# Layer 1's way in by token halves, idle products on TensorE, and two scan pairs of WKV 1 at another place

## The reference

```python
ek = exp(min(k, 30)); ekv = ek * v          # k = v = fside, the same for all layers
a = a * decay + ekv_t; b = b * decay + ek_t # scan over tokens, forward and in reverse
num = nf + nb - ekv + euk * vf              # euk = exp(min(u + k, 30))
den = df + db - ek + euk
out = sigmoid(r) * (num / max(den, 1e-8)) * (0.8 + 0.2 * tf)   # r = x
```

## Time and profile before

| | us |
|---|---|
| median of 3 runs (519.27 to 520.88) | 520.41 |
| profiled execution | 519.72 |
| its span, first to last instruction | 517.8 |
| PE busy | 437.8 (85%) |
| DVE busy | 377.9 (73%) |
| ACT busy | 195.2 (38%) |
| POOL busy | 108.0 (21%) |
| mean granted PE clock | 0.924 of 2.4 GHz |

### The profile page before, as it was taken

The page is one execution under the profiler, slowest core; times in us unless marked ns, Lnnn a source line. Parts: engine busy times, 40 slices in busy tenths (PEclk is TensorE's granted clock), DMA queues, the critical chain, the costliest instruction groups (busy, mean ns, idle before and its releaser), DMA issues.

```text
span 517.8 us, 5641 instructions
## 1 busy us (share of the span) xinstructions
PE 437.8 (85%) x2006; PEld 269.3 (52%) x2006; DVE 377.9 (73%) x663; ACT 195.2 (38%) x339; POOL 108.0 (21%) x65
## 2 busy tenths in 40 slices
PE   0796789987670899999999999999999999987572
PEld 0342444776470377899998997534434434322120
DVE  4999888797899798768666686375566773347975
ACT  4450155652221486321544824250010030146481
POOL 0000000000000297322000000047466654350000
PEclk9998788998965599999999999899999999999695
DMA  7910000710192127744754239020000000000001
GB/s 294 416 48 1 1 0 0 288 69 1 43 327 76 44 53 234 236 130 162 203 184 160 85 128 332 6 84 0 0 0 1 1 0 0 0 0 1 1 26 55
DMA packets 12093, 47.76 MB, mean 92 GB/s; under 512 B 2866, under 2 KB 5147, under 8 KB 9763
## 3 DMA queue, kind: packets, MB, share of 16 engines
q1 hardware_dynamic: 10914, 43.48, 24.0%
q0 software_dynamic: 1152, 3.93, 3.1%
HBM read 45.04 MB, written 2.37 MB: 92 GB/s over the span
## 4 chain that ended last, share of the span: by engine, by line
PE 69%; DVE 22%; issue 3%; ACT 3%; DMA 3%; SPq 0%; DVEq 0%
PE bank L1417 9%; PE bank L1391 8%; PE bank L1506 7%; PE bank L1515 7%; PE bank L1426 5%; PE bank L1543 3%; PE bank L1546 3%; PE bank L1279 3%; DMA const<-in_const 3%; PE bank L1321 2%; PE bank L1340 1%; PE bank L1311 1%; PE bank L1482 1%; DVE arena L903 1%; PE bank L1383 1%
## 5 line engine op out<-in xcount | busy, mean ns | idle before, releaser
L568 ACT ACTIVATE early<-bank 128x512 f32<-128x512 f32 (+1 forms) x24 | 14.3, 596 | 98.5 <-PE bank L1515 90.4
L1133 DVE TENSOR_TENSOR early<-early,bank 128x512 f32<-128x512 f32 (+1 forms) x24 | 16.4, 684 | 48.0 <-ACT early L568 47.6
L1391 PE MATMUL bank<-onehot,rows 128*128 128x512 f32 x192 | 51.4, 406 | 0.0
L341 POOL DMA_INDIRECT arena<-token_rows,arena x24 | 35.6, 1484 | 70.4 <-DVE arena L921 36.9
L1417 PEld LDWEIGHTS bank<-arena 128*96 128x96 f32 x512 | 44.2, 165 | 4.0 <-issue 3.9
L1506 PE MATMUL bank<-cT,arena 128*128 128x512 f32 (+1 forms) x96 | 46.2, 606 | 0.0
L1515 PE MATMUL bank<-arena 128*128 128x512 f32 (+1 forms) x96 | 45.8, 596 | 0.1
L1417 PE MATMUL bank<-arena 128*96 128x48 f32 x512 | 44.8, 248 | 0.3 <-issue 0.3
L1391 PEld LDWEIGHTS bank<-onehot,rows 128*128 128x128 f32 x192 | 33.9, 189 | 6.1 <-DVE onehot L952 0.3
L354 POOL TENSOR_TENSOR early<-early,arena 128x512 f32<-128x512 f32 (+1 forms) x12 | 28.0, 2333 | 41.8 <-DVE early L1133 41.8
L352 POOL TENSOR_TENSOR early<-early,arena 128x512 f32<-128x512 f32 (+1 forms) x12 | 15.1, 1262 | 103.0 <-DMA arena<-pair_weights 98.1
(11 more groups left out here) (315 smaller groups left out, 869.2 us busy)
## 6 DMA issues: line engine op xcount, KB each, us to landing
arena<-in_w_gate SPq DMA_DIRECT2D x8, 768.0 KB, 4.8
arena<-in_w_up SPq DMA_DIRECT2D x8, 768.0 KB, 7.8
arena<-in_w_down SPq DMA_DIRECT2D x8, 768.0 KB, 9.5
const<-in_const SPq DMA_DIRECT2D x1, 2122.5 KB, 13.1
arena<-in_wq SPq DMA_DIRECT2D x1, 2048.0 KB
arena<-in_wo SPq DMA_DIRECT2D x1, 2048.0 KB, 9.3
kT<-in_kT SPq DMA_DIRECT2D x2, 512.0 KB, 5.3
xT<-in_xT SPq DMA_DIRECT2D x1, 1024.0 KB, 8.5
```

What stands on the lines that cost most here:

```text
L341: g.indirect_dma_start(xg[:, t % XRING, :], None, scratch[:, :], bass.IndirectOffsetOnAxis(ap=toki[:, t:t + 1].bitcast(U32), axis=0)).then ...
L1391: return mm(bank[2 * ct + ch][:], rows1[:, i % RRING, part, ct * P:(ct + 1) * P], onehot1[:, t, ch * CHUNK:(ch + 1) * CHUNK], start=False, ...
```

## The change

- `scalar`: `gate(l)` becomes `gate0()` (as before) and `gate1()`, which makes four sigmoids of 512 columns, token half by token half, each as soon as its addition is done.
- `vector`: `cond(1)` (two products of 1024 columns behind the four additions) becomes four `cond1(i)` of 512 columns; the first stands behind the third addition, the others behind the fourth. The additions go by token halves. `ratio_ready` is waited for ahead of them.
- `tensor`: the scatter goes by token halves; two idle products of 512 columns into bank 5 follow it. The logits wait for `c_ready` 2 for tokens 0 to 511 and 4 for the rest, instead of for all at once; the wait for `x1_ready` stands behind the logits.
- `tensor`: three idle products into bank 6 behind the QKV bias products; the definition of `idle` moves to the block's head.
- `vector`: `num_scans(1, 0, 0)` and `(1, 0, 1)` move from in front of the selected rows' copy to behind `den(1, 1)`.
- `vector`: the residual `x1` is added straight from bank 4, and the copy `ao` is made behind its sum of squares.
- Layer 2's waits on `sig_ready` and `c_ready` count two more.

```diff
--- before.py
+++ after.py
@@ -395,13 +395,17 @@
-            def gate(l):
+            def gate0():
+                act.wait_ge(S("x_in"), 16)
                 for ct in range(CT):
-                    if l == 0:
-                        act.wait_ge(S("x_in"), 16)
-                    else:
-                        act.wait_ge(S(f"x{l}_ready"), 2 * ct + 2)
                     s.activation(cT[:, ct, :], xT[:, ct, :], ACT.Sigmoid).then_inc(S("sig_ready"), 1)
...
+            def gate1():
+                for i in range(4):
+                    ch, ct = divmod(i, 2)
+                    cc = slice(ch * CHUNK, (ch + 1) * CHUNK)
+                    act.wait_ge(S("x1_ready"), i + 1)
+                    s.activation(cT[:, ct, cc], xT[:, ct, cc], ACT.Sigmoid).then_inc(S("sig_ready"), 1)
@@ -424,7 +428,7 @@
             euk(0)
-            gate(0)
+            gate0()
             for j in range(4):
@@ -474,7 +478,7 @@
-            gate(1)
+            gate1()
             act.wait_ge(S("logit1_done"), 1)
@@ -667,11 +671,11 @@
-            def cond(l):
-                dve.wait_ge(S("ratio_ready"), l)
-                for ct in range(CT):
-                    dve.wait_ge(S("sig_ready"), 2 * l + ct + 1)
-                    v.tensor_tensor(cT[:, ct, :], cT[:, ct, :], ratio[l % 2][:, ct, :], ALU.mult).then_inc(S("c_ready"), 1)
+            def cond1(i):
+                ch, ct = divmod(i, 2)
+                cc = slice(ch * CHUNK, (ch + 1) * CHUNK)
+                dve.wait_ge(S("sig_ready"), CT + i + 1)
+                v.tensor_tensor(cT[:, ct, cc], cT[:, ct, cc], ratio[1][:, ct, cc], ALU.mult).then_inc(S("c_ready"), 1)
@@ -744,8 +748,6 @@
             den_sum(1, 1)
-            num_scans(1, 0, 0)
-            num_scans(1, 0, 1)
@@ -771,6 +773,8 @@
             den(1, 1)
+            num_scans(1, 0, 0)
+            num_scans(1, 0, 1)
             cosb = cs[:, 0:64].unsqueeze(1).to_broadcast([P, 8, 64])
@@ -817,9 +821,9 @@
             dve.wait_ge(S("wo_done"), 1)
-            step(v.tensor_copy(ao, bank[4][:, 0:C]))
-            step(v.tensor_tensor(x1, xs, ao, ALU.add))
+            step(v.tensor_tensor(x1, xs, bank[4][:, 0:C], ALU.add))
             sumsq(x1, 6)
+            v.tensor_copy(ao, bank[4][:, 0:C])
             dve.wait_ge(S("rms0"), 2)
@@ -843,13 +847,17 @@
+            dve.wait_ge(S("ratio_ready"), 1)
             for i in range(4):
-                ct, ch = divmod(i, 2)
+                ch, ct = divmod(i, 2)
                 dve.wait_ge(S("scatter0_done"), i + 1)
                 xx = xT[:, ct, ch * CHUNK:(ch + 1) * CHUNK]
-                v.tensor_tensor(xx, xx, bank[i][:], ALU.add).then_inc(S("x1_ready"), 1)
...
-            cond(1)
+                v.tensor_tensor(xx, xx, bank[2 * ct + ch][:], ALU.add).then_inc(S("x1_ready"), 1)
+                if i == 2:
+                    cond1(0)
+            cond1(1)
+            cond1(2)
+            cond1(3)
             last_tokens(wD)
@@ -1045,7 +1053,7 @@
                     cc = slice(ch * CHUNK, (ch + 1) * CHUNK)
-                    dve.wait_ge(S("sig_ready"), 2 * CT + 2 * ct + ch + 1)
+                    dve.wait_ge(S("sig_ready"), 3 * CT + 2 * ct + ch + 1)
                     v.tensor_tensor(cT[:, ct, cc], cT[:, ct, cc], ratio[0][:, ct, cc], ALU.mult).then_inc(S("c_ready"), 1)
@@ -1199,6 +1207,11 @@
+            def idle(bk, n):
...
+                for _ in range(n):
+                    mm(bank[bk][:], ident, iota[:, 0:CHUNK], start=True, stop=True)
...
             def tokens_to_rows(banks, layer):
@@ -1243,6 +1256,7 @@
                 qkv_bias(j)
+            idle(6, 3)
             pe.wait_ge(S("rank_ready"), 1)
@@ -1327,19 +1341,20 @@
             pe.wait_ge(S("dl_ready"), 1)
-            for ct in range(CT):
-                for ch in range(NCH):
+            for ch in range(NCH):
+                for ct in range(CT):
                     mm(bank[2 * ct + ch][:], dl[:, ct * P:(ct + 1) * P], onehot[:, ch * CHUNK:(ch + 1) * CHUNK],
...
-            pe.wait_ge(S("c_ready"), 2)
-            pe.wait_ge(S("x1_ready"), 4)
+            idle(5, 2)
             pe.wait_ge(S("small1_in"), 80)
             for i in range(NT):
+                pe.wait_ge(S("c_ready"), i // 4 * 2 + 2)
                 for ct in range(CT):
...
             last.then_inc(S("logit1_done"), 1)
+            pe.wait_ge(S("x1_ready"), 4)
             tokens_to_rows([0, 1, 2, 3], 1)
@@ -1435,11 +1450,6 @@
                 last.then_inc(S("outtr_done"), 1)
...
-            def idle(bk, n):
...
-                for _ in range(n):
-                    mm(bank[bk][:], ident, iota[:, 0:CHUNK], start=True, stop=True)
@@ -1582,11 +1592,11 @@
             pe.wait_ge(S("w2a_in"), 112)
-            pe.wait_ge(S("c_ready"), 3)
+            pe.wait_ge(S("c_ready"), 5)
             z2(0, 0)
...
             for half in range(2):
-                pe.wait_ge(S("c_ready"), 5 + half)
+                pe.wait_ge(S("c_ready"), 7 + half)
                 logits2(half)
```

## The result

| | before | changed |
|---|---|---|
| median | 519.99 us (4 runs, 519.27 to 520.88) | 530.63 us (4 runs: 523.58, 530.35, 530.92, 532.79) |
| profiled execution, its span | 519.72, 517.8 | 530.92, 528.6 |
| mean granted clock | 0.924 | 0.906 |
| PE busy | 437.8 (85%) | 449.2 (85%) |

The ratio is 1.0162 [1.0117, 1.0207]; forecast were 516.3 us and a range of 514.2 to 518.9. Ratios leave out runs over 1.5% above a kernel's fastest as disturbed; here that upper level is itself what the change brings, so I also give medians over all runs, and how many lie at 526 us or above.

A forecast was written before the change was run, and what follows sets the result against it. It took PE (69%) and DVE (22%) alternating up to 183 us, then nearly all PE, as the bound. 3.2 + 0.3 + 0.87 - 0.3 = 4.1 us off 519.72 gave 515.6, median 516.3; range 514.2 to 518.9.

The forecast's parts named there:

- what is won earlier moves that part as a block: From 183 us on, nearly all PE and unedited: time won earlier shifts this whole part with it.
- PE early wins nothing there and PE late costs: At 183 us, gather and shared products' end coincide: earlier PE gains nothing, each us of later clock rise costs 0.5.
- Bounds 0 and 3.6: Loss if the clock rises later under the last eight shared passes at 183 us: 0 to 3.6 us, taken as 0.3.
- rival (c): Early idle products late and QKV at 1.2 GHz beyond 5.6 us: slower, 522.2 us at 10 us; chance 0.06.
- The early idle products: In PE's hole before the rank product: clock holds, one-hots start 0.2 us earlier, row selection 0.8 us shorter.
- the bound named beside it: Early idle products at 1.2 GHz: they take 5.1 us, end at 60.9, and everything on DVE is 2.8 later.
- Rival (b): Early idle products don't hold the clock: 520.0 us at worst, 518 with most at 2.4 GHz; chance 0.17.
- The scans: Two WKV 1 scan pairs moved: with the early idle products 3.2 us gained up to attention, between 2.2 and 4.2.
- The residual: Layer 0, add reads the bank, its 0.42 us copy moves behind: gain 0.3 us, between 0 and 0.42.
- The way in: Scatter to layer 1's routing: logits 3.5 us instead of 6.99, stage gains 0.87 us, bounds 0.5 and 0.9.
- The pieces: Layer 1 gating on DVE: two 512-column pieces cost what one of 1024 did, against the skill's some 0.3 us more.

The follow-up runs named there:

- c2: Changed kernel plus twelve idle products: seven before the routing weights' wait, three at the expert loop's entry, one in each of the first two groups; median 524.40 us.
- i1: e2_no_early plus twelve idle products: seven before the routing weights' wait, three at the expert loop's entry, one in each of the first two groups; median 519.92 us.
- s1_scans: Kernel before, with only the two scan pairs moved and the residual read from the bank; median 517.22 us, ratio 0.9947.
- s3_early: Kernel before, with only the three idle products behind the bias products added; median 534.19 us.
- e2_no_early: Changed kernel without the three idle products ahead of the rank product; median 527.93 us.
- t1_wait1: e2_no_early with the routing's first addition done twice, 0.75 us more; median 517.37 us, ratio 0.9939.

## Why the prediction was wrong, point by point

- **The step that failed:** "what is won earlier moves that part as a block", said of all that comes behind 183 us, and with it "At 183 the first gather and PE's shared products arrive together …, so PE early wins nothing there and PE late costs", with "Bounds 0 and 3.6 …; I take 0.3". PE early was taken as free at worst. It idled 1.81 us for the gather, and the part behind did not move as a block: the first group alone took 12.03 us more, at half clock. I priced a late rise and never an early one, though two rows were there to price it: the second shared passes, whose four took as long as the eight behind them (3.67 and 3.60), and a first group of 5.61 that takes twice that at half clock. The range had no term for it, so it could not hold the time. My argument against rival (c), that no dense stretch there stayed low beyond 5.6 us, looked at the earlier trace rows alone: the logits ran 6.99 us at half clock in my own rows. That a low clock can last under dense work was there to be seen.
- **The early idle products**, "I take the gain, since PE no longer stops": wrong, and the bound named beside it was right. They ran at half clock, 5.25 us against "5.1 us". That the rank product came at 60.83 (bound: 60.9) is an accident of the start: on the common scale it is 15.89 against a bound of 14.7, for the bias products had ended 1.16 later than in the trace I worked from. Rival (b) had this mechanism. The tables were then 2.65 later on the common scale, where (b) said 0.5: the 1.16 is a part of it, and (b) counted on a faster row selection; that took 5.38, not 3.6. c2 less i1 puts the products at 4.5 us in most runs. I had read the hole of 2.36 us off one trace; others have none.
- **The scans**, "I take 3.2" with the idle products, between 2.2 and 4.2: mis-sized. Seven profiled versions have the scans moved and no early idle products. They reach the first maximum 48.54 to 50.81 us after the common point (s1_scans 49.43), seven with this part as before 50.18 to 51.46: 1.3 us earlier on the mean. With the scans gone DVE waits for PE's row selection in front of the copy, which took 4.25 to 5.61 us in those seven and not the 3.6 I counted on, so the copy comes 0.3 to 1.7 us earlier and not 2.4.
- **The residual:** forecast 0.3, measured 0.45 (2.25 less 1.80), just over the upper bound of 0.42.
- **The way in:** scatter to routing 14.55 before, 13.61 after, 0.94 gained against "0.87"; logits 3.76 against 3.5; the rest of PE's gain went into its idling in front of the routing's product (12.78 us instead of 7.55), as written. What I had not asked is what those 0.94 us would trigger 30 us later.
- **The pieces:** by the Trainium skill, "VectorE: DVE Perf Modes", on the TRN2 errata, two more DVE instructions would cost some 0.3 us (an estimate from its figure of about 150 cycles). The trace agrees for single instructions: 0.69 us for 512 columns and 1.22 for 1024, so two pieces hold 0.16 more. But DVE starts the next one before that: pieces start 0.60 apart (three in 1.89), 1024-column ones 1.13 apart (two in 2.35), so a piece more costs 0.07. The row I decided by showed less than that, because the second of its two gatings started only 1.21 after the first.
- **Rival (c)** forecast slower for another reason, QKV at half clock for longer. QKV started 2.75 later and the maximum only 2.29 later, so it was not that.

**Shown:** the place (first group at half clock), the gap in front of it in each of the six traces that lost the clock there, that with the gap filled the first group keeps full clock, that time added ahead removes the upper level and other time added brings it. **Not shown:** what sets the moment of the rise in a single run, and why two traces kept the clock over a gap of the same length. Most versions have runs at more than one level. The Trainium skill, "TensorE: Matmul & The Clock Gate", Part 1, says that the window of activity by which the clock is set runs freely and doesn't start anew with the kernel; this would give one program two levels, but no run here shows that window. Open too are why s3_early, whose shift lies far upstream, is so often at the upper level, and the 0.85 us pause and the fall behind it in the second group.

## What to carry to other kernels

Before you move a stage, ask what arrives early: an engine that now comes first idles in front of a transfer that hasn't moved. Here the price on TensorE was not the gap but the clock of the stretch behind it. Price that stretch at both clock levels and let the range hold it. Before you fill a hole with idle work, see in several executions whether it is always there. Judge such a kernel by many runs and by how many lie at each level, and test a suspected alignment by adding a fraction of a microsecond ahead of it: if the kernel gets faster, that speaks for the alignment.

## What the runs showed of the hardware

- A gap of 1.8 us in front of the expert products goes with a clock of 0.50 from 184 to 210 us, PE busy 24.0 of 24 us between 184 and 208. Unless a gap or a pause comes, the same products at 1.00 stay at 1.00. The same shape twice: 5.61 and 10.39 us. The kernel before has a low stretch of this kind too: 0.50 from 142 to 152 us, with PE busy 10.0 of 10 us on the logits and the transposes behind them.
- Added 512-column products in a hole ran at 1.2 GHz, 1.75 us each in front of the rank product, and at 2.4 GHz, two in 1.88, behind the scatter and at the entry: the same product cost 1.75 or 0.94 us, by the clock granted where it stood.
- One kernel, unchanged, ran at 518 to 521, at 522 to 525 and at 530 us; the share at 526 and above went from 9 of 128 to 8 of 10 with this change, and from 9 of 13 to 0 of 12 with 0.75 us of work added to it (e2_no_early, t1_wait1).
